# A mixture-of-experts router: its paced scatters become bursts with waits, and the keys of a later layer move behind the slot table

## The reference, cut to what matters

```python
x = x + _L0_xattn_ref(_layernorm(x), ctx, ctx, mask0, ...)      # 16 heads
x = x + _L0_ffn_ref(_layernorm(x), gate_w, fc_w, proj_w)        # 8 experts, top 2, gelu
x = x + _L1_xattn_ref(...)                                      # one head, biases on q, k, v
x = x + _L1_ffn_ref(...)                                        # 8 experts, top 2, relu
x = x + _L2_xattn_ref(...)
x = x + _L2_ffn_ref(...)                                        # quantised linear, depthwise convolution
x = x + _L3_xattn_ref(..., mask3, ...)
x = x + _L3_ffn_ref(...)                                        # 8 experts, top 2, silu(g) * u
```

## Time and profile before

| what | us |
|---|---|
| three runs | 592.61, 595.84, 595.80 |
| their median | 595.8 |
| the profiled execution | 592.61 |
| its span, first to last instruction | 590.9 |
| first expert block, first to last step on TensorE | about 95 to 182 |

### The profile page before, as it was taken

One profiled execution on the slowest core, in us unless ns is written; L12 is line 12 of the kernel. 1 busy time (PEld: TensorE's weight loads), 2 busy tenths in 40 slices (PEclk: granted clock), 3 DMA queues, 4 the chain that ended last, 5 costly groups with the idle time before them and its releaser, 6 DMA issues.

```text
span 590.9 us, 12314 instructions
## 1 busy us (share of the span) xinstructions
PE 542.1 (92%) x3808; PEld 455.7 (77%) x3809; DVE 405.7 (69%) x1443; ACT 238.3 (40%) x551; POOL 281.3 (48%) x521
## 2 busy tenths in 40 slices
PE   5999999978897899999998999989997799999992
PEld 3677767967796599888986867757784399999992
DVE  8988876322267895456679899988888575665573
ACT  3455525434454444343343233445541133333330
POOL 4374268888758107900000031546426688774332
PEclk9999768999999899989999999999999699999997
DMA  9998113322253100000000360004000222221334
GB/s 301 379 334 259 44 45 87 76 66 71 73 166 106 61 1 1 2 0 1 1 2 0 115 172 1 1 2 144 1 1 28 60 70 64 64 67 45 84 108 124
DMA packets 48152, 47.65 MB, mean 81 GB/s; under 512 B 6470, under 2 KB 37603, under 8 KB 47942
## 3 DMA queue, kind: packets, MB, share of 16 engines
q1 hardware_dynamic: 43558, 37.68, 21.6%
q0 software_dynamic: 4544, 9.38, 4.9%
HBM read 27.53 MB, written 19.51 MB: 80 GB/s over the span
## 4 chain that ended last, share of the span: by engine, by line
PE 75%; DVE 18%; issue 3%; ACT 2%; DMA 1%; another core or an unknown queue 0%; DVEq 0%; POOL 0%; POOLq 0%; ACTq 0%; SPq 0%
PE bank L2424 18%; PE bank L2437 11%; PE bank L2000 8%; PE bank L2241 4%; PE bank L2280 4%; PE bank L2196 3%; PE bank L2269 2%; PE bank L1989 2%; PE bank L1990 2%; PE bank L1991 2%; PE bank L2412 1%; PE bank L1960 1%; PE bank L1880 1%; PE bank L2338 1%; DVE zmax L1210 1%
## 5 line engine op out<-in xcount | busy, mean ns | idle before, releaser
L2424 PE MATMUL bank<-xT,wcur 128*128 128x128 f32 x936 | 119.6, 278 | 9.8 <-ACT xT L895 6.6
L2424 PEld LDWEIGHTS bank<-xT,wcur 128*128 128x128 f32 x936 | 111.0, 192 | 14.4 <-issue 11.0
L705 POOL DMA_INDIRECT yt<-Y,dest_i x62 | 61.1, 986 | 47.6 <-ACT Y L911 25.5
L644 POOL TENSOR_SCALAR var_eps<-mv 128x4 f32<-128x4 f32 (+2 forms) x12 | 2.9, 238 | 169.7 <-DVEq L1821 95.1
L689 POOL DMA_INDIRECT xw<-XW,slot_i x64 | 63.4, 990 | 24.5 <-issue 11.1
L1447 DVE COPY wcur<-WA 128x512 f32 x78 | 36.6, 471 | 53.0 <-PE bank L2424 23.0
L979 ACT ACTIVATE hT<-bank,b_cols 128x512 f32<-128x512 f32 x64 | 44.0, 688 | 62.4 <-PE bank L1991 61.8
L2000 PE MATMUL bank<-WC,hT 128*128 128x128 f32 x512 | 64.0, 280 | 0.0
L2000 PEld LDWEIGHTS bank<-WC,hT 128*128 128x128 f32 x512 | 61.6, 195 | 1.4
L1591 DVE SCALAR_TENSOR_TENSOR X<-bank,G,X 128x128 f32<-128x128 f32 x128 | 36.0, 344 | 32.5 <-PE bank L2000 28.7
L1462 DVE TENSOR_TENSOR hT<-gb,bank 128x512 f32<-128x512 f32 x39 | 26.8, 687 | 41.4 <-ACT gb L900 33.9
(11 more groups left out here) (405 smaller groups left out, 1190.3 us busy)
## 6 DMA issues: line engine op xcount, KB each, us to landing
xw<-pad_rows SPq DMA_DIRECT2D x34, 260.0 KB, 4.2
xrow<-xw SPq DMA_DIRECT2D x78, 65.0 KB
WA<-in_fc_dram SPq DMA_DIRECT2D x16, 256.0 KB, 4.7
YT<-yt SPq DMA_DIRECT2D x16, 256.0 KB, 2.9
WA<-in_pj_dram SPq DMA_DIRECT2D x8, 256.0 KB, 6.1
WB<-in_fc_dram SPq DMA_DIRECT2D x8, 256.0 KB, 4.7
WB<-in_pj_dram SPq DMA_DIRECT2D x8, 256.0 KB, 6.5
X<-in_x_dram SPq DMA_DIRECT2D x2, 512.0 KB, 4.4
```

What stands on the lines that cost most here:

```text
L705: pool.indirect_dma_start(out=yt_dram, out_offset=bass.IndirectOffsetOnAxis(ap=dest_i[:, t:t + 1], axis=0), in_=y_slot(layer, t), in_offse ...
L2424: ins = pe.matmul(dst, wcur[:, s4, at:at + P], xT[s4 % 2][:, :], start=True, stop=True)
```

## The change

It has two parts.

- The scatters of layer 0 have no pauses any more. In their place the first scatter of groups 1, 4 and 6 waits until the group before has landed (before, only group 1 did). Layer 1 keeps what it had: the wait at group 1 and the pauses from group 3 on. The puts keep their pauses in both layers.
- In layer 0 `later_keys` is moved behind `later_m(2)` and `later_m(3)`, on TensorE and on ScalarE; on TensorE it was ahead of the table. The wait for all copies of M moves from the first second product to ahead of the first transpose.

```diff
@@ constants
+BURSTS = ((1, 4, 6), (1,))
-UNPACED = (1, RING - 1)
@@ GpSimd, experts(layer)
                 for group in range(1, last + (layer == 0)):
-                    if group == 1:
-                        pool.wait_ge(scattered[0], landed(layer, 0))
+                    if group in BURSTS[layer]:
+                        pool.wait_ge(scattered[(group - 1) % RING], landed(layer, group - 1))
                     if group >= RING:
                         pool.wait_ge(scattered[group % RING], landed(layer, group - RING))
                     if layer and group == RING - 1:
                         pool.wait_ge(ex_xc, SLOTS + 1)
                     for tile in range(MOVED[group], MOVED[group + 1]):
                         for choice in range(TOPK):
-                            if group >= UNPACED[layer]:
+                            if layer and group >= RING - 1:
                                 pause()
                             scatter(layer, group, tile, choice)
@@ ScalarE
             router(1)
-            later_keys()
             for b in range(GB, B):
                 later_m(b)
+            later_keys()
             experts(0)
@@ TensorE, router
-                if layer == 0:
-                    later_keys()
                 table(layer)
                 if layer == 0:
                     later_m(2)
                     later_m(3)
+                    later_keys()
@@ TensorE, dn_mm of experts
-                    if first:
-                        pe.wait_ge(m_evac, 2 * B)
-                    else:
+                    if not first:
                         pe.wait_ge(ex_y, t + (base - 1))
@@ TensorE, ahead of the first transpose
                 if layer == 0:
-                    pe.wait_ge(m_evac, B + 2)
+                    pe.wait_ge(m_evac, 2 * B)
                     pe.wait_ge(s1_evac, 8)
```

## The result

The changed kernel takes 600.96 us in the median of 5 runs (598.14 to 606.27) against 595.8 for the kernel before (592.61 to 596.6, 5 runs): a ratio of 1.011, 95% interval 1.0069 to 1.0151. Ratios here compare all fast runs of both kernels, so they aren't the quotient of the two medians (1.009). The forecast was no change, 595.8 us, in a range up to 599.5. The profiled execution has a span of 600.3 us where that of before had 590.9; TensorE is busy for 3.1 us more, and the rest of the difference is waiting.

What follows compares the result with a forecast made beforehand. TensorE, busy for 92% of the span, was taken as the bound, so gains must come from its own waits. A shorter slow stretch (-1.3 us) and later keys (+1.3) summed to 0.0: 595.8 us, range 585.5 to 599.5.

Steps and rivals of the forecast that it cites:

- The scatters' timing: GpSimd, layer 0: 22 scatters at 1.26 us plus two new waits of 1.27 put the first put at 117.0, 4.2 us earlier.
- at 117.0 TensorE has done 10.1 steps: First expert block: from 97.2 to the first put at 117.0 TensorE's steps were assumed to take 1.96 us each.
- The third rival: Slow hand-over begins with the unpaused scatters: 2.52 us per step from 97.2, net +2.1 us, 597.9; chance 0.15.
- no step ran beside them: Argument against slow hand-overs beside dense scatters: group 0's ten scatters had that period already, but without TensorE steps beside them.
- The slow stretch: TensorE steps of 2.79 us during layer 0's puts: predicted to last 32.1 us instead of 36.6, a gain of 1.3 us.
- the first rival: The stretch of slow TensorE steps doesn't come back: 10.9 us won, 1.3 lost, -9.6 in all, 586.2; chance 0.2.
- one late slot taken away: Possible reason for the slow steps to vanish: a late slot triggers them and earlier scatters remove it; 10.9 us won.
- The keys: Router, keys behind `later_m`: first transpose at 93.1, first second product at 97.2 instead of 95.91; cost 1.3, bounds 0.7 to 3.0.
- No load waits longer than before: SyncE's loads of slots 9, 13, 17: group 4's last scatter issued by 100.3 (was 102.6), the last of all by 116.7 (120.9).
- -1.3 + 1.3: Whole kernel: 1.3 us gained from a shorter run of slow steps, 1.3 lost to the later start; sum 0.0.

Runs made afterwards that it cites:

- e7: Kernel before with no pauses at layer 0's scatters or puts, no added landing waits, keys in their old place; ratio 1.0137 to the kernel before.
- e0: Kernel before, only with SyncE's load of the landing counts keeping its run-time bounds test, as every experiment does; ratio 0.9987 to the kernel before.
- quick group: Runs made together on one chip, first and fourth of five such sets; there the unchanged kernel took 582.95 and 582.87 us in the median.
- slow group: Runs made together on one chip, second, third and fifth of five such sets; there the unchanged kernel took 596.52, 603.54 and 604.78 us.
- e10: Kernel before with a second pause behind each of the first 24 puts of layer 0; ratio 1.0108 to the kernel before.
- e1: Kernel before with the keys' part of the change alone, scatters keeping their pauses; ratio 1.0026 to the kernel before.
- e14: The whole change with the pauses ahead of layer 0's 22 scatters put back, late keys and added landing waits kept; ratio 1.0062 to the kernel before.
- e2: Kernel before with the scatter part of the change alone, keys staying ahead of the table; ratio 0.9967 to the kernel before.
- e3: Kernel before with the scatter part alone and without its two added landing waits; ratio 0.9905 to the kernel before.
- e12: Kernel before with half the elements in every pause (96 instead of 192), in both layers; ratio 0.9945 to the kernel before.
- e13: Kernel before with a pause ahead of only every second of layer 0's 22 scatters; ratio 0.9938 to the kernel before.
- e5: The whole change against the kernel before, run again on another chip; ratio 1.0104.
- e8: Scatter part of the change alone against the kernel before, repeated where the unchanged kernel took 603.54 us; ratio 1.0124.
- e16: The whole change against the kernel before, once more, where the unchanged kernel took 604.78 us; ratio 1.0065.
- e18: Kernel before with a pause ahead of only every second scatter of layer 0, repeated where the unchanged kernel took 604.78 us; ratio 1.0070.
- e9: Keys' part of the change alone against the kernel before, repeated where the unchanged kernel took 603.54 us; ratio 1.0020.

## Why the prediction was wrong

**The scatters' timing: right.** First put predicted at 117.0, measured at 117.23; the last scatter's end at 116.7 against 116.93 (115.97 + 0.96); each new wait 1.4 to 1.5 us over the usual gap of 0.30, where 1.27 was taken. It just didn't pay: of the 4 us won on GpSimd none reached TensorE.

**The step that failed** is "at 117.0 TensorE has done 10.1 steps". It had done three. The working kept the pace of before, 1.96 us, for steps that now ran beside unpaced scatters. From the first to the fifth second product 21.8 us passed (102.18 to 123.94), 5.4 us per step. The third rival, the slow hand-over beginning with the unpaced scatters, was the right mechanism with the wrong size. It let each hand-over wait for the next gap, 2.52 us per step; in fact a gap of 0.30 us lets mostly nothing through, and the signal waits for a landing wait or the end of the burst (not always: e7 has results taken up within its burst, at 99.71 and 101.11, 5.6 and 0.8 us late). The evidence in the earlier trace rows (result taken up just ahead of the next put) was read rightly, and then the mechanism was given a chance of 0.15 because the earlier trace rows shows layer 1 without it. Layer 1 does have late hand-overs, up to 2.1 us in the trace of before (a product over at 492.88, taken up at 495.46); its steps of 2.79 us have room for them. And "no step ran beside them", said of the ten unpaced scatters of group 0, passed over the keys: their end at 85.38, just behind the last of these scatters, was taken up 1.5 us late, where e0, in a quick group, has 0.03 (85.28, taken up at 85.31).

**The slow stretch: wrong, and the first rival right in part.** It didn't come back: 1.91 us per step behind 124. The reason is less pleasant than the rival's "one late slot taken away": TensorE was so far behind that the puts waited for results, and puts that wait leave long gaps. As far as these traces show, the stretch isn't a property of the puts but of GpSimd working off a backlog with a single pause between two of them, in a slow group. The last window of after (37.6 us of GpSimd's 62) and e10 (backlog, two pauses, full pace) show it from both sides. It paid back 14.2 us where the rival had 10.9, since outside that stretch too the steps of before had taken 1.95 to 1.99 us and now take 1.91.

**The keys: the place right, the size wrong.** First second product predicted at 97.2, bounds up to 3.0 us behind 95.91; measured 6.3 behind. In the trace after, ScalarE hears of the keys 3.57 us late (predicted: at once; bound: 1.5), and then the three first products run at a granted clock of 0.53, nearly all of it at the lower level: from first transpose to first second product it takes 6.0 us and not 4.05. e1 has the second of these alone, and e14 neither. In after TensorE had stood idle from 91.8 to 96.1, in e1 only for 0.88 us, as in e14; what decides between e1 and e14 these rows don't show. The earlier trace rows had shown 0.50 only for the 1.2 us ahead of the first products, and the working assumed that it would be over by then. The working also took the keys' 1.26 us, at a mean clock of 0.81, as if at the upper level (it gave 1.85 us; the trace after has 1.51). The range should have carried the 3 us or so that three first products at the lower level cost. But what this is worth by itself is little: 1.0026 and 1.0020, since TensorE's later start is paid back at slot 17 or in the slow stretch, as the prediction had it for other waits.

**"No load waits longer than before": true of GpSimd's times, and a missed lever.** In the first trace TensorE was held up by late signals and never reached slot 17 early. In the quick groups it did, and there the load, not the puts, is what earlier scatters are worth.

Sum: predicted -1.3 + 1.3. Measured in the block +6.27 (late start) + 14.18 (steps two to five) - 14.24 (slow stretch and rest) = +6.21. Faster by 0.3% to 1% was measured for e2, e3, e12 and e13 in quick groups alone; each kind of denser scatter that was run in a slow one (e5 to e8, e16, e18) lost 0.65 to 1.4%. e3 and e12 were not run in a slow group, the whole change not in a quick one. No version that was run in both beats the kernel before in both.

What stays open: why TensorE's signals are held up in some groups and not in others; whether it is the writing of descriptors or the traffic behind it that holds them; and what sets the block's end at 187 to 190 us in eight traces of the slow groups (e5 to e9, e16 to e18), however the delay is spread; the second, third and fifth group have no trace of the kernel before. So the traces place the delay, and how much of it reaches the end of the kernel is known from the first result and the ratios alone.

## What to carry to other kernels

Read who releases a wait: where the work named was over for microseconds and the row says "remote" or "issue", the signal is the cost, and the engine whose instructions fill just that time is the first to look at. A pause that looks like waste may be the gap that other engines' signals need; before taking it out, price a hand-over that waits for the end of the burst and not for the next gap. And measure such a change on more than one chip: here the same edit, the scatter part, is worth -0.3% (e2) or +1.2% (e8), depending on where it runs.

## What was not expected of the hardware

- A product of TensorE was taken up by ScalarE and VectorE over 19 us after its end, ScalarE standing idle for the last 14.5 of them, while GpSimd issued indirect DMAs 0.30 us apart (e7), and within 0.1 us on another chip with the same kind of burst (e3). TensorE followed ScalarE's signals within 0.1 us in the same stretch of e7 (101.39 to 101.44), within 0.3 in the changed kernel. The Trainium skill (SBUF — State Buffer, "Who interferes with whom") speaks of a port pair shared by VectorE and GpSimd; ScalarE, which by that page waits for nobody's port, was late like VectorE, so by that page this is something else.
- The unchanged kernel took 583 us in two groups and 597 to 605 in the three others, and the late hand-overs came with the higher ones: none in 8 traces of the quick groups, in each of the 12 others (with the two of the first measurement).
- TensorE's granted clock at the start of the steps differs between executions with nearly the same instructions and times: 0.50 from 94 to 98 us in e1, 1.00 in e14, with TensorE busy in both. The first second product starts 3.5 us later in e1; 0.9 of that stands already at the first transpose (93.51 against 92.64), the other 2.6 lie in the products at the lower level, and no wait explains them.
